# Estimates of one DMA queue instead of two, and new weights, in the step order of the softmax attentions of a two-layer decoder

## The reference

```python
def _mha(x, y, wq, wk, wv, ...):              # 16 heads of 32
    q = jnp.einsum('bsc,hcd->bhsd', _ln(x, ...), wq)
    k = jnp.einsum('btc,hcd->bhtd', _ln(y, ...), wk)
    v = jnp.einsum('btc,hcd->bhtd', _ln(y, ...), wv)
    a = jax.nn.softmax(jnp.einsum('bhsd,bhtd->bhst', q, k) * D ** (-0.5), axis=-1)
    if causal: a = a * mask
    o = jnp.einsum('bhst,bhtd->bhsd', a, v)
    ...
x = x + _mha(x, x, ..., causal=True)          # tag a1, 512 keys
return x + _mha(x, ee, ..., causal=False)     # tag a2, 1601 keys
```

## Time and profile before

| | us |
|---|---|
| median of 3 runs | 3887.3 (3878.41 to 3892.47) |
| the profiled execution | 3892.38, its span 3891.1 |
| PE, DVE, ACT, POOL busy | 3393.8, 2249.4, 1675.6, 981.0 |
| mean granted clock of TensorE | 0.929 |

### The profile page before, as it was taken

One profiled execution on the slowest core, in us unless ns is written; L12 is line 12 of the kernel. 1 busy time (PEld: TensorE's weight loads), 2 busy tenths in 40 slices (PEclk: granted clock), 3 DMA queues, 4 the chain that ended last, 5 costly groups with the idle time before them and its releaser, 6 DMA issues. The chain is left out here.

```text
span 3891.1 us, 59054 instructions
## 1 busy us (share of the span) xinstructions
PE 3393.8 (87%) x22156; PEld 2132.0 (55%) x22156; DVE 2249.4 (58%) x4065; ACT 1675.6 (43%) x3067; POOL 981.0 (25%) x1030
## 2 busy tenths in 40 slices
PE   6789999999997957788867799999999987899998
PEld 3444444444435834455446555555555536787787
DVE  5768677686771366545445776676766615433432
ACT  1116657566573222334432255555455644222222
POOL 1110000000001023333334255555555553100000
PEclk9979999999998977899888799999999998999999
DMA  2022212212212215444420634343434302122211
GB/s 70 6 51 54 64 48 51 58 47 65 50 37 107 76 43 86 67 65 62 58 71 31 79 57 66 58 62 54 66 53 65 54 18 77 51 82 71 66 55 59
DMA packets 144627, 229.42 MB, mean 59 GB/s; under 512 B 40916, under 2 KB 90840, under 8 KB 141400
## 3 DMA queue, kind: packets, MB, share of 16 engines
q1 hardware_dynamic: 129048, 216.21, 26.9%
q10 hardware_dynamic: 15296, 9.45, 1.0%
HBM read 99.39 MB, written 8.91 MB: 28 GB/s over the span
## 5 line engine op out<-in xcount | busy, mean ns | idle before, releaser
L1104 DVE TENSOR_REDUCE a_mp<-bank 128x1 f32<-128x384 f32 (+2 forms) x1280 | 685.3, 590 | 400.0 <-PE bank L954 399.5
L1062 ACT ACTIVATE a_p<-bank 128x512 f32<-128x512 f32 (+1 forms) x1088 | 584.4, 600 | 514.7 <-PE bank L979 346.4
L1104 DVE TENSOR_REDUCE mx_mp<-bank 128x2 f32<-128x768 f32 (+4 forms) x640 | 588.7, 953 | 181.0 <-PE bank L954 105.0
L1062 ACT ACTIVATE mx_p<-bank 128x512 f32<-128x512 f32 (+3 forms) x1088 | 541.8, 558 | 318.0 <-PE bank L979 176.2
L1140 POOL TENSOR_TENSOR a_pair<-a_p 128x512 f32<-128x512 f32 x384 | 489.9, 1311 | 460.0 <-ACT a_p L1062 370.5
L954 PE MATMUL bank<-a_ks,a_qs 126*128 126x384 f32 (+2 forms) x1280 | 455.2, 397 | 52.6 <-ACT a_v L1985 22.3
L979 PE MATMUL bank<-a_qs,a_ks 128*128 128x512 f32 (+1 forms) x1088 | 468.0, 446 | 22.5 <-DVE a_yn L1860 5.3
L260 POOL TENSOR_TENSOR rs<-ve,neghalf 128x4 f32<-128x4 f32 (+2 forms) x80 | 78.3, 979 | 1098.8 <-DVE ve L255 1055.2
L979 PEld LDWEIGHTS bank<-a_qs,a_ks 128*128 128x128 f32 (+1 forms) x1088 | 206.6, 193 | 255.9 <-issue 169.2
L979 PE MATMUL bank<-mx_qs,mx_ks 64*128 64x512 f32 (+3 forms) x1088 | 304.1, 466 | 36.4 <-DVE mx_vc L1377 15.4
L954 PEld LDWEIGHTS bank<-a_ks,a_qs 126*128 126x128 f32 x1280 | 250.8, 197 | 132.7 <-DVE a_mp L1104 30.0
(11 more groups left out here) (311 smaller groups left out, 5580.0 us busy)
## 6 DMA issues: line engine op xcount, KB each, us to landing
sf_raw<-in_h_w SPq DMA_DIRECT2D x64, 512.0 KB, 3.5
a_ks<-a_kh SPq DMA_DIRECT2D x96, 192.0 KB, 4.5
ex_w<-in_L_ffn_w SPq DMA_DIRECT2D x16, 1024.0 KB, 5.1
a_qs<-a_qh SPq DMA_DIRECT2D x64, 256.0 KB, 6.9
mx_ks<-mx_kh SPq DMA_DIRECT2D x192, 48.0 KB, 2.1
a_ks<-a_kl SPq DMA_DIRECT2D x48, 192.0 KB, 5.2
mx_qs<-mx_qh SPq DMA_DIRECT2D x128, 64.0 KB, 2.2
mx_rec<-mx_flat SPq DMA_DIRECT2D x128, 64.0 KB, 2.0
```

The lines of the kernel that those rows point to most:

```text
L1062: act.activation(probs[place % len(probs)][0:kp, q0:T], self.bank(part, n, kb, h)[0:kp, q0:T], ACT.Exp, scale=scale).then_inc(*self.frees( ...
L1104: v.tensor_reduce(best[:, tiled * j:tiled * j + tiled, i, ci], bank[:, 0:w] if tiled == 1 else bank[:, :, 0:w], AX.X, ALU.max).then_inc(*s ...
```

## The change

`Pace.transfer` keeps one queue for the transfers of both issuing engines instead of one for each; the bytes count 0.0078 ns each instead of 0.0098, the landing 1100 ns instead of 900. The weights of a1 (`OWN`) and one weight of a2 (`CROSS`) get new numbers; those of `mx` (`MIXED`) stay.

```diff
-ISSUE, SENT, LANDING = {"sp": 610, "act": 500}, 0.0098, 900
+ISSUE, SENT, LANDING = {"sp": 610, "act": 500}, 0.0078, 1100
 Policy = namedtuple("Policy", "act_ahead dve_ahead values more_values totals more_totals search early_search turn stack beside aging rate lead")
 MIXED = Policy(700, 1100, 350, 200, -160, 140, -50, 600, 50, 60, 200, 100, 2.6, 4)
-OWN = Policy(700, 1100, 300, 200, -210, 90, 100, 600, -250, 60, 200, 100, 4.2, 2)
-CROSS = Policy(700, 1600, 300, 200, 90, 40, 100, 600, 50, 110, 200, 50, 5.2, 2.5)
+OWN = Policy(700, 1100, 300, 200, -160, 190, 150, 600, 200, -90, 200, 30, 4.2, 2.5)
+CROSS = Policy(700, 1600, 300, 200, 90, 40, 100, 600, 50, 110, 200, 30, 5.2, 2.5)
...
     def transfer(self, engine, size, ready):
         issued = self.run(engine, ISSUE[engine], ready)
-        self.free["queue", engine] = max(self.free["queue", engine], issued) + size * SENT
-        return self.free["queue", engine] + LANDING
+        self.free["queue"] = max(self.free["queue"], issued) + size * SENT
+        return self.free["queue"] + LANDING
```

## The result

The changed kernel takes 3824.1 us (median of 4 runs, 3820.0 to 3829.7) against 3888.4 for the kernel before; the ratio is 0.9839 with a 95% interval of 0.9815 to 0.9864, so 64 us or 1.6% faster. The forecast was 3840 with a range of 3808 to 3878. Once more beside other kernels the changed one took 3826.2, ratio 0.9847 (0.9828 to 0.9865).

The account below looks back on a forecast made before the run. The prediction saw a1 as the loose stage: PE idle 90.0 us, waiting on DVE and ACT held by a late small transfer. Gaps 39 plus clock 12 made 51 us off 3892.4, about 3840; range 3808 to 3878.

Parts of the forecast that it names:

- The cause and its place: In a1, ten PE gaps end just behind a reciprocal whose small gather waits behind six 256 KB copies; 48.8 us together.
- The gaps: In a1, later `inverse` and `flat` win 80% of PE's 48.8 us of gaps: 39 us, bounds 0 and 48.8.
- The clock: In a1, PE's granted clock no longer drops behind each gap: 12 us won, bounds 0 and 30.
- The weights of a1: New planner weights in a1, chiefly `turn` and `stack`, give 0 us; at most 20 us won.
- The hidden work: In a1, peaks and exponentials fill the 7 to 10 us before `inverse` and `flat`; about 0.5 us of wait left.
- a2: Second cross stage, 1058 us: truer estimates bring no new waits; change 0 us, bounds 8 us either way.
- Rival 1: In a1, gaps move to DVE's backlog or the next stack; half stay, no clock regained: 3868 us, chance 0.17.
- Rival 2: `thin` lands late for another reason, or mx and a2 lose what a1 gains: 3888 us, no change, chance 0.13.
- Rival 3: In a1, turned maxima leave after the next six copies and wait behind them: 3921 us, 29 us slower, chance 0.08.

Follow-up runs that it names:

- small copies: Kernel before, its order and waits kept; later a1 query and key copies carry only an eighth of their columns: a1 429.5 us, kernel 3829.3 us.
- the fixed delay: Kernel before with two queues; only in a1 `inverse`, and with it `flat`, planned 6.5 us later: a1 447.0 us, ratio 0.9902.

## Why the prediction held, point by point

- **The cause and its place: right.** Ten gaps of PE in a1, traced to 8 KB that wait behind 1.5 MB of the other engine's; the shared estimate alone takes 56.5 us out, small copies in the old order take out as much (53.5), and both without a new weight.
- **The gaps, 39 of 48.8 us: right in size.** PE idles 42.3 us less, and 38.0 less with the shared queue alone.
- **The clock, 12 us: too small.** PE is busy 22.6 us less. I had 30 as the bound and took 40% of it because other engines would set the pace; once the gaps are gone the granted clock is at 1.00 in every stretch of 30 us from 1530 to 1860, and three quarters came (18.5 us with the shared queue alone). In part this can be scatter: with the maxima alone shared, almost the order of the kernel before, PE is busy for 394.1 us, 4.9 less than before. This term is most of the 14 us by which the sum (51) missed a1 (65 in the one pair, 62 against the repeated run).
- **The weights of a1, 0 us: too small.** With the queue true they bring 5 to 8 us (426.2 against 418.0 and 421.2), by `turn`, within the 20 that I allowed. That gain is part of the 42.3 and the 22.6 us above and does not come on top of them. Without the queue they bring nothing, by way of the third rival. My working names `lead`, which goes from 2 to 2.5, only in that rival; no run moves it alone.
- **The hidden work: half right.** I expected `inverse` and `flat` to stand where they can run, with 0.5 us of wait left, and DVE's wait to fall to 25 us. It is 45.6, with single waits of 5 us. What counts is what stands behind the wait: the reciprocal has moved behind the split of the maxima, and 5 us in front of nothing cost nothing. I also treated ACT's wait and DVE's as one; the run with `flat` alone late shows that DVE's is enough to keep PE idle, and leaves ACT's share open.
- **a2, 0 with bounds of 8: right for the whole change, wrong for a part.** I wrote that the changed estimates should bring no new waits. The shared queue alone costs a2 13.5 us in one profile and 9.6 in another with the same order; the constants give most of it back, and some 3 us stay. The old queue's 0.0098 ns a byte counts the three copies of a key cut at 7.3 us where 6.4 are measured, and shared it puts this excess before ACT's small transfers too. That this is the mechanism is argued, not shown.
- **Rival 1** (the gaps move to other waits) is seen only in part kernels, as 8.8 us for the maxima with the fixed delay and, with `flat` alone late, 15.7 us for the maxima and 14.2 for the peaks. **Rival 2** falls: the reciprocal follows the gather in 2.15 us instead of 7.33 when the copies are small, and mx and a2 together changed by 2 us. The rule of the Trainium skill on turn-taking between rings ("DMA: Bandwidth & Descriptors", "Queues, rings and completion order") does not foretell the time of a small transfer here; its sentence on the completion increment fits. What it is that waits behind the copies, the small transfer's own packets or only its completion increment, no run here shows. **Rival 3** is real and worth 19.1 us of PE's waits with the weights alone, where the estimate is blind to the shared path; with the whole change PE waits only 0.6 us for them in a1, as the edit counts that delay.

## What to carry to other kernels

In a hand-made or planned order, look behind each wait, not at it: the 5.05 us that DVE waits in the changed kernel with nothing urgent queued behind cost nothing, and the 5.09 us in front of the last peak and the split cost PE 5.43. In this kernel the transfers of the two issuing engines are one path for the time at which things land (before the change, 8 KB issued 0.3 to 4.2 us after the other engine's last 256 KB copy were used 6.8 to 10.6 us after their issue); a small transfer ordered right after large ones is best planned as if it were the last of them. And correct the model before the weights: the same new weights were worth nothing with the false queue and 5 to 8 us with the true one.

## What the runs showed of the hardware that was not expected

A gap of 3 to 9 us costs TensorE more than its length: in a1 the busy time fell by 22.6 us with 42.3 us of idle time removed, and by 18.5 with 38.0 when only the queue was shared, about half a microsecond for each one. The granted clock of the stage went from 0.89 to 0.97 in both.

Executions of one order differ by stage. DVE, ACT and POOL run mx in one order in the kernel before and in eight of the others, and it took from 1001.4 to 1011.3 us; the kernel before has the longest. a1 took 418.0 and 421.2 in two executions of the changed kernel. So a difference of 5 us, in mx of 10, between single profiles of a stage tells nothing by itself.
